# A selective-scan layer on one core: the last batch scanned as one unit of 1024 tokens instead of two units of 512

## The reference

```python
x = x + conv_block(ln(x))                 # a mamba block, per batch
# inside: xz = x_norm @ in_proj.T ; xi, z = split ; causal conv of 4 taps ; u = silu(.)
#         dt, Bm, Cm = split(u @ x_proj.T) ; delta = softplus(dt @ dt_proj.T + b)
def step(h, inp):                         # over the 1024 tokens of a batch
    u_t, d_t, B_t, C_t = inp
    dA = exp(d_t[..., None] * A)          # 128 channels x 16 states
    h = dA * h + (d_t * u_t)[..., None] * B_t[:, None, :]
    y = einsum('bdn,bn->bd', h, C_t)
    return h, y
#         y = (y + u * D) * silu(z) ; y @ out_proj.T + skip * x_norm ; layer norm ; projection
t = tokens(x)
# then a mixture of 8 experts with a capacity of 640 tokens each:
#   logits -> argmax expert, its softmax weight, position = running count in that expert
#   tokens are put into (expert, position) rows, each expert applies relu(x w1 + b1) w2 + b2,
#   and the result, times the weight, is added to the token
x = t + ffn(ln(t))
```

## Time and profile before

| what | us |
|---|---|
| median of 3 executions | 444.93 (444.12 to 445.0) |
| the profiled execution | 444.72 |
| its span | 443.0 |
| batch 2, from its first drive to the first drive of batch 3 | 182.67 to 257.45 |
| half unit 1 | 257.45 to 297.49 |
| half unit 2, to the end of its last scan | 297.49 to 336.86 |
| from there to the first scatter of the last tiles | 336.86 to 358.29 |
| the first expert product on PE | 369.38 |

### The profile page before, as it was taken

One profiled execution on the slowest core, in us unless ns is written; L12 is line 12 of the kernel. 1 busy time (PEld: TensorE's weight loads), 2 busy tenths in 40 slices (PEclk: granted clock), 3 DMA queues, 4 the chain that ended last, 5 costly groups with the idle time before them and its releaser, 6 DMA issues. The chain is left out here.

```text
span 443.0 us, 3907 instructions
## 1 busy us (share of the span) xinstructions
PE 312.3 (70%) x1137; PEld 169.0 (38%) x1137; DVE 321.4 (73%) x359; ACT 207.1 (47%) x340; POOL 266.3 (60%) x205
## 2 busy tenths in 40 slices
PE   1844398756899894399987578886677678888600
PEld 0321143213645352174534254333233535566500
DVE  4037999999999997999796997899595130566810
ACT  1435747772567684654859147454251202443100
POOL 7024766679466657688566679558666030467772
PEclk9968599996689996959999688988898579999855
DMA  5992988986578874489795247877870009000000
GB/s 135 168 165 86 382 321 280 291 298 216 201 255 293 302 281 163 134 273 290 264 300 162 72 125 162 291 233 179 215 233 9 15 12 240 7 5 21 24 6 0
DMA packets 44416, 78.74 MB, mean 178 GB/s; under 512 B 16433, under 2 KB 22408, under 8 KB 44394
## 3 DMA queue, kind: packets, MB, share of 16 engines
q1 hardware_dynamic: 41434, 73.88, 54.8%
q0 software_dynamic: 2960, 4.61, 4.4%
HBM read 72.29 MB, written 7.68 MB: 181 GB/s over the span
## 5 line engine op out<-in xcount | busy, mean ns | idle before, releaser
L418 POOL TENSOR_TENSOR prod<-h,csb 128x1024 f32<-128x1024 f32 (+1 forms) x80 | 155.2, 1947 | 81.6 <-DVE h L995 60.4
L785 PE MATMUL Yp<-prod,ident 128*128 128x512 f32 x256 | 138.4, 665 | 35.3 <-POOL prod L418 35.2
L995 DVE TENSOR_TENSOR_SCAN h<-dA,Bp 128x1024 f32<-128x1024 f32 (+1 forms) x64 | 128.8, 2016 | 4.1 <-POOL prod L418 0.8
L579 ACT ACTIVATE dA<-delta,aneg 128x1024 f32<-128x1024 f32 (+1 forms) x80 | 76.8, 972 | 56.5 <-DVE h L995 29.2
L785 PEld LDWEIGHTS Yp<-prod,ident 128*128 128x128 f32 x256 | 48.4, 208 | 96.7 <-POOL prod L418 58.5
L973 DVE TENSOR_TENSOR Bp<-Cp,bsb 128x1024 f32<-128x1024 f32 x48 | 59.2, 1232 | 1.7
L447 POOL DMA_INDIRECT slots<-rows_,slot x32 | 33.3, 1041 | 22.8 <-DVE slot L1063 14.9
L473 POOL DMA_INDIRECT out_dram<-dA,h x20 | 20.2, 1010 | 25.9 <-DVE dA L1151 21.0
L1137 DVE TENSOR_TENSOR dA<-M,b2s 128x320 f32<-128x320 f32 x8 | 3.9, 491 | 31.0 <-PE M L912 31.0
L980 DVE TENSOR_TENSOR Bp<-Cp,bsb 128x1024 f32<-128x1024 f32 x16 | 19.7, 1233 | 8.7 <-DMA bsb<-bc_rows 7.6
L995 DVE TENSOR_TENSOR_SCAN h<-dA,hl,Bp 128x512 f32<-128x512 f32 x16 | 20.2, 1274 | 2.1 <-POOL prod L418 1.4
(11 more groups left out here) (214 smaller groups left out, 485.8 us busy)
## 6 DMA issues: line engine op xcount, KB each, us to landing
bsb<-bc_rows SPq DMA_DIRECT2D x48, 512.0 KB, 5.3
csb<-bc_rows SPq DMA_DIRECT2D x48, 512.0 KB, 5.5
bsb<-bc_rows SPq DMA_DIRECT2D x32, 256.0 KB, 4.7
csb<-bc_rows SPq DMA_DIRECT2D x32, 256.0 KB, 4.1
slots<-fill POOLq DMA_DIRECT2D x1, 2600.0 KB, 18.3
h<-slots SPq DMA_DIRECT2D x4, 325.0 KB, 4.2
csb<-slots SPq DMA_DIRECT2D x3, 325.0 KB, 5.7
xs_in<-in_x_dram SPq DMA_DIRECT2D x1, 768.0 KB, 10.0
```

What stands on the lines that cost most here:

```text
L418: po.tensor_tensor(prod[:, k % 4, c], h[:, k % 3, c], csb[:, k % CSLOTS, c], ALU.mult).then_inc(s_pP, 1)
L579: ac.activation(dA[:, k % 3, c], delta[:, c], ACT.Exp, scale=aneg[:, n:n + 1]).then_inc(s_dA, 1)
L785: ins = te_.matmul(Yp[:, HB[q]], idn, prod[:, k % 4, HB[q]], start=False, stop=(n == 15), skip_group_check=True)
L995: ve.tensor_tensor_scan(h[:, k % 3, c], dA[:, k % 3, c], Bp[:, :] if whole else Bp[:, HB[n % 2]], hl[:, n:n + 1] if v == CARRY + 1 else 0. ...
```

## The change

Batch 3 becomes one unit of 8 tiles like the others, so V = 4. `drive_pair`, `carry`, the buffer `hl`, its semaphore and the waits on it go. Nothing else is edited, but everything that goes by `UNITS` changes with it: the batch's 32 scans, products and exponentials of 512 tokens become 16 of 1024, its 64 row loads of 256 KB become 32 of 512 KB, and the work behind the last scan (`back(V-1)` and `scatter(V-1)`) is for 8 tiles instead of 4.

```diff
-UNITS = [(b, 0, T) for b in range(B - 1)] + [(B - 1, 0, T // 2), (B - 1, T // 2, T // 2)]
+UNITS = [(b, 0, T) for b in range(B)]
 V = len(UNITS)
-CARRY = V - 2
...
-            def carry(n):
-                k = N * CARRY + n
-                act.wait_ge(s_scan, k + 1)
-                ac.activation(hl[:, n:n + 1], h[:, k % 3, HALF - 1:HALF], ACT.Copy).then_inc(s_hl, 1)
...
-            def drive_pair(v, n):
-                k, c = N * v + n, span(v)
-                dve.wait_ge(s_scan, k)
-                for i in (k, k + 1):
-                    dve.wait_ge(b_in[i % CSLOTS], 16 * (i // CSLOTS + 1))
-                ve.tensor_tensor(Bp[:, :].rearrange("p (n l) -> p n l", n=2),
-                                 Cp[:, c].unsqueeze(1).broadcast_to([P, 2, HALF]),
-                                 bsb[:, k % CSLOTS:k % CSLOTS + 2, c], ALU.mult).then_inc(s_mul, 2)
-
             def scan(v, n):
                 k, c = N * v + n, span(v)
-                whole = UNITS[v][2] == T
                 if k >= 3:
                     dve.wait_ge(s_pP, k - 2)
-                if N * CARRY <= k - 3 < N * (CARRY + 1):
-                    dve.wait_ge(s_hl, k - 3 - N * CARRY + 1)
-                if v == CARRY + 1:
-                    dve.wait_ge(s_hl, n + 1)
                 dve.wait_ge(s_mul, k + 1)
                 dve.wait_ge(s_dA, k + 1)
-                ve.tensor_tensor_scan(h[:, k % 3, c], dA[:, k % 3, c], Bp[:, :] if whole else Bp[:, HB[n % 2]],
-                                      hl[:, n:n + 1] if v == CARRY + 1 else 0.0, ALU.mult, ALU.add).then_inc(s_scan, 1)
-                if n + 1 < 16 and whole:
+                ve.tensor_tensor_scan(h[:, k % 3, c], dA[:, k % 3, c], Bp[:, :], 0.0, ALU.mult, ALU.add).then_inc(s_scan, 1)
+                if n + 1 < 16:
                     drive(v, n + 1)
-                if n + 1 < 16 and not whole and n % 2:
-                    drive_pair(v, n + 1)
```

More of the change, by code:

```diff
@@ L156, in metaformer_layer @@
         cg = sb("cg", [P, T, C])
-        hl = sb("hl", [P, N])
         n2 = sb("n2", [P, T, C + 1])
@@ L208, in metaformer_layer @@
              "f_dt f_am f_abs f_exp f_one f_ln f_sq f_less f_high f_pick f_delta f_du").split())
-        s_mul, s_dA, s_scan, s_pP, s_sum, s_hl = map(sem, "s_mul s_dA s_scan s_pP s_sum s_hl".split())
+        s_mul, s_dA, s_scan, s_pP, s_sum = map(sem, "s_mul s_dA s_scan s_pP s_sum".split())
         (b_yg, b_op, b_sq, b_y2, b_var, b_rs, b_n2, b_tr, b_n2T, b_pr, b_t1, b_tr3, b_h3T, b_lg, b_cg, b_var3, b_rs3,
@@ L656, in _ @@
                 decay(v, 0)
-                if v == CARRY + 1:
-                    carry(N - 1)
                 decay(v, 1)
@@ L662, in _ @@
                         decay(v, n + 2)
-                    if v == CARRY and n:
-                        carry(n - 1)
                     if v and n < 8:
@@ L1116, in _ @@
                 dve.wait_ge(f_du, UNITS[v][0] + 1)
-                if UNITS[v][2] == T:
-                    drive(v, 0)
-                else:
-                    drive_pair(v, 0)
+                drive(v, 0)
                 for n in range(16):
```

## The result

| | before | after |
|---|---|---|
| median of 20 executions | 444.31 us | 448.96 us |
| lowest to highest | 442.01 to 446.94 | 443.70 to 452.57 |
| ratio after / before | | 1.0065 (1.0035 to 1.0095) |
| profiled execution, its span | 444.72, 443.0 | 451.12, 449.4 |

The change makes the kernel slower, by 0.35 to 0.95%. The forecast was 445.9 us in a range of 440.5 to 450.5, slower with a chance of 0.50. The sign held and the size was too small: the sum said +1.2, the medians say +4.65, which lies within the wide range and outside the forecast's own 444 to 448. Every ratio leaves out the executions that lie more than 1.5% above the fastest of their kernel, here the three longest of the changed kernel (451.12, 451.49 and 452.57) and further down five of the light filling's twelve, while the medians are of all executions; the two medians in the table stand 1.0% apart.

A forecast was written before the change was run, and what follows sets the result against it. DVE was taken to bound the scans and a chain of dependent steps the tail; −17.4 + 15.0 + 5.15 − 2.0 + 0.4 = +1.2 us on 444.72 gave 445.9 us, range 440.5 to 450.5.

The forecast's parts named there:

- the sum: Whole kernel: −17.4 + 15.0 + 5.15 − 2.0 + 0.4 = +1.2 us, giving 445.9 us.
- the two regimes: DVE sets the pace of the scans; the tail behind the last scan is one chain from engine to engine.
- Term 1: Batch 3's scan stretch, first drive to last scan: 79.4 us falls to 62.0, a gain of 17.4.
- The front's three waits: Batch 2's scans: DVE waits 6.1 us on work delayed by `front`; these go in batch 3.
- rival 1: Batch 3's scans: DVE's waits come back elsewhere, up to 6.1 us, giving 452 us; chance 0.11.
- Term 2: Tail from last scan to first scatter: eight tiles for four add 15.0 us, making 36.4.
- Rival 3: Tail: clock already at half at the last sum, +4.7 us, giving 450.6 us; chance 0.10.
- Rival 2: Tail: the clock stays full, 7.8 us less, giving 438.1 us; chance 0.12.
- Term 3: Last scatter: four more scatters in line, about 1.29 us each, add 5.15 us.
- Term 4: Before the first expert: unused products already hid 2.0 us of the scatters' delay, −2.0; a possible clock fall adds +0.4.

The follow-up runs named there:

- light filling: Changed kernel plus unused wide products in PE's gaps of the tail, none before the last sum: 452.09 us, ratio 0.9925 to the kernel before.
- second profile: Changed kernel run again unaltered on another chip: profiled execution 446.05 us; median 451.73 against 446.7 for the kernel before, ratio 1.0077.

## Why the prediction was right, and where its sizes were off

- **What bounds the two regimes: right.** DVE is busy 60.22 of 61.80 us in the scans, and nothing is near full in the tail.
- **Term 1, −17.4: measured −17.6**, 61.80 us in the changed kernel against the 62.0 forecast, and 61.78 to 61.80 in every kernel with whole units. The front's three waits went, as assumed, and rival 1 is refuted: no wait of DVE is left. The parts hold too: DVE was busy 62.16 of batch 2's 69.87 us and is busy 60.22 of 61.80 now, so 1.9 us of its own work went (1.7 forecast) and 6.1 us of waiting (6.1 forecast). What the trace adds is where it came from: DVE's own work falls by only 66.59 − 60.22 = 6.4 us (34.22 + 32.37 in the earlier trace rows), and 11.2 us are waits and gaps of the half units, of which 5 to 6 are the B rows behind C rows.
- **Term 2, +15.0: measured +16.0 and +18.7.** The main step that was mis-sized is the last sum with the skip's and output's products. I let four sums run at the full clock because batch 2's pace would keep it. It did not: the clock falls in the sum in both profiles, behind a wait of 2.08 us for the last whole product, and the sum takes 3.02 and 3.18 us. The output's products should end 8.9 us behind the last scan (5.4 before, +1.2 and +2.25); they end 10.0 behind it in the second profile and 12.7 in the first. All that follows them was right: forecast 36.4 − 8.9 = 27.5 us up to the first scatter, measured 27.41 and 27.43. So the doubling of transposes, projection, centering and logits at half clock holds to 0.1 us as a sum; its single steps were not all checked.
- **Rival 3, clock already at half at the last sum, had 0.10** and said +4.7 on the sum. That is nearly the case of the first profile, where the skip's and output's products took 3.67 and 3.67, and the tail was 3.8 over the forecast's 36.4. The argument for it, that PE has gaps at the last states, was the right one. It was given too small a chance: before, the four instructions of the last two sums had taken 3.72 us, the half clock's length.
- **Rival 2, the tail keeps the full clock: refuted** for the changed kernel. The granted clock is 0.50 from 328.7 or 321.8 on. The Trainium skill, page "TensorE: Matmul & The Clock Gate", section "Part 1: The HAM clock gate", has the fall come after an idle stretch. Whether the trace agrees is open for the fall at 321.8: PE had waited 2.08 us before it, and the fall went when PE was kept at work, but a wait of 2.05 us at 310.3 was followed by none. The trace does not agree for the fall at 328.7, before which PE had been busy for 7.5 us. The rival's price was sized well: 7.8 us forecast, 7.5 measured when wide products held the clock, the fillers' own cost included.
- **Term 3, +5.15: measured 367.60 − 358.62 = 8.98 for 3.86, +5.12.**
- **Term 4, −2.0: right.** Terms 3 and 4 without the clock make +3.15; the first expert stands 14.21 behind the first scatter for 11.09, +3.12, and 14.31 in the second profile. The clock at the first expert, +0.4 in bounds of 0 to 2.6, is 0 in one profile and 2.6 in the other. I sized a case with two outcomes as a small mean, and that is the second mis-sized step.
- **The sum, +1.2,** is met by the second profile (+1.3), and that is in part luck: it is one execution, the shortest of its six, on a chip whose kernel before was 2.4 us longer at the median, and term 2 is 1.0 too small even there, which the start of batch 3 (−0.6) and the clock at the first expert (0 for +0.4) make up. The difference of the medians is missed by 3.4 us. By the stages it holds a worse clock case in more than half of the executions; both together make +5.4.

What stays open: why one execution keeps the clock at the two places and another not. The waits there are alike (2.08 us ahead of the last sum in both; 2.48 us ahead of the first expert with a full clock, 1.97 with a half one), so the length of the wait alone does not decide. That the twelve long executions are those with the clock down at one or both places is inferred from two profiles and the mean clocks; it was not seen in each.

## What to carry to other kernels

Splitting the last unit costs something in the scans (here 17.6 us, of which 6.4 are the bound engine's own work and the rest waits and gaps), and it takes half of the finish out of the chain behind it, where that half was worth 18.1 us at like clock. The two nearly cancel, so the sign hangs on small things. Before weighing such a split, look at what the smaller units wait for: here 5 to 6 of the 17.6 us were a queue's order, which two moved lines mend. In a chain of short dependent steps the clock is a term like any other: look for the gap ahead of its first step, and price it as two outcomes, not as a mean.

## What the runs showed of the hardware that was not expected

- TensorE's clock fell to half behind unbroken work. In the second profile of the changed kernel it fell at about 328.7, when PE had worked since 321.19 without a gap, the last 4.4 us in 64-column products, and stayed there for the next 27 us with PE busy 16.8 of them. In the light filling it came back during the third of three 512-column products in a row. In the second profile it also came back in the middle of the skip's thin products, behind the last sum's wide ones.
- The same program draws different clocks at the same place: the skip's products took 2.43 and 3.67 us in two profiles with equal waits ahead of them.
- The indirect scatters on POOL's queue stood 1.28 us apart (0.97 and 0.30 of issue) in all kernels, and the last one of the changed kernel's first profile landed 2.15 us after its issue.
- Profiles of the same code differed by 1.3 us in a stretch of scans: with B rows ahead the half units took 73.19 us at a granted clock of 0.91 and 74.45 at 0.84.
